# A two-layer pair kernel on one core: the second layer's projections in four row tiles, three blocks a set, with masking, channel order and output constants moved

## The reference, cut to what matters

```python
zn = _layernorm(z, ln_in_w, ln_in_b)
a = m * sigmoid(zn @ a_g_w.T + a_g_b) * (zn @ a_p_w.T + a_p_b)
b = m * sigmoid(zn @ b_g_w.T + b_g_b) * (zn @ b_p_w.T + b_p_b)
x = einsum('bikh,bjkh->bijh', a, b)
xn = _layernorm(x, ln_out_w, ln_out_b)
gate = sigmoid(zn @ g_w.T + g_b)
out = gate * (xn @ z_w.T + z_b)
```

## Time and profile before

| | us |
|---|---|
| Median of 3 runs | 320.16 |
| Lowest and highest | 319.91, 321.51 |
| The profiled execution | 320.25 |
| Its span in the trace | 318.4 |
| PE busy | 248.8 (78%) |
| DVE busy | 241.3 (76%) |
| ACT busy | 218.5 (69%) |
| POOL busy | 128.0 (40%) |

### The profile page before, as it was taken

One profiled execution on the slowest core, in us unless ns is written; L12 is line 12 of the kernel. 1 busy time (PEld: TensorE's weight loads), 2 busy tenths in 40 slices (PEclk: granted clock), 3 DMA queues, 4 the chain that ended last, 5 costly groups with the idle time before them and its releaser, 6 DMA issues.

```text
span 318.4 us, 7162 instructions
## 1 busy us (share of the span) xinstructions
PE 248.8 (78%) x2296; PEld 200.1 (63%) x2296; DVE 241.3 (76%) x543; ACT 218.5 (69%) x986; POOL 128.0 (40%) x140
## 2 busy tenths in 40 slices
PE   0597750589999999999999999998755977758710
PEld 0587320467778777887788787776555656658710
DVE  6058950578899888998989988887349479968994
ACT  1546650399998999998999989997445755426700
POOL 6670000045455455544554454555000365630562
PEclk9999595599999999999999999999758799978775
DMA  9100132635344354433544333410000462000017
GB/s 140 32 0 2 50 71 35 234 138 198 125 162 155 106 185 165 152 128 130 182 151 171 128 127 123 146 38 2 2 0 0 170 250 78 3 0 2 0 21 127
DMA packets 44041, 31.29 MB, mean 98 GB/s; under 512 B 23108, under 2 KB 44004, under 8 KB 44004
## 3 DMA queue, kind: packets, MB, share of 16 engines
q1 hardware_dynamic: 43004, 30.70, 30.5%
q10 hardware_dynamic: 1000, 0.13, 0.3%
HBM read 1.38 MB, written 1.18 MB: 8 GB/s over the span
## 4 chain that ended last, share of the span: by engine, by line
PE 64%; DVE 15%; DMA 6%; ACT 5%; issue 5%; SPq 2%; DVEq 0%; ACTq 0%
PE psum L1083 10%; PE psum L1135 10%; PE psum L1146 9%; PE psum L1086 5%; PE psum L1084 5%; PE psum L1115 5%; DMA maps<-mask_parts 4%; DVE tok L781 3%; PE psum L1001 3%; PE psum L979 2%; PE psum L1103 2%; PE psum L1204 2%; PE psum L1123 2%; DVE tok L836 2%; DMA maps<-in_x 2%
## 5 line engine op out<-in xcount | busy, mean ns | idle before, releaser
L497 POOL TENSOR_TENSOR probs<-probs,rden 96x384 f32<-96x384 f32 x96 | 79.0, 823 | 122.4 <-DVE rden L919 122.4
L645 ACT ACTIVATE probs<-psum,neg_max 96x96 f32<-96x96 f32 x384 | 124.1, 348 | 2.4 <-PE psum L1135 0.5
L645 ACT ACTIVATION_READ_ACCUMULATOR probs<-psum,neg_max 96x1 f32 x384 | 82.5, 215 | 0.0
L913 DVE COPY probs_t<-psum 96x384 f32<-96x384 f32 x96 | 52.9, 551 | 20.2 <-PE psum L1135 18.8
L882 DVE TENSOR_REDUCE neg_max<-psum 96x4 f32<-96x384 f32 x96 | 50.8, 529 | 2.0 <-PE psum L1086 2.0
L1083 PE MATMUL psum<-u_st,x_stack 128*96 128x384 f32 x96 | 40.5, 422 | 14.5 <-DMA u_st<-u_split 13.8
L1135 PE MATMUL psum<-ident,probs 96*96 96x96 f32 x384 | 47.7, 246 | 1.1 <-DVE probs_t L913 0.9
L1135 PEld LDWEIGHTS psum<-ident,probs 96*96 96x96 f32 x384 | 37.7, 126 | 5.4 <-issue 1.4
L1146 PE MATMUL psum<-probs_t,v_sb 128*32 128x96 f32 x768 | 35.8, 258 | 0.0
L1083 PEld LDWEIGHTS psum<-u_st,x_stack 128*96 128x96 f32 x96 | 15.7, 164 | 28.2 <-issue 14.0
L1086 PE MATMUL psum<-bias_lo,ident_r 128*96 128x384 f32 x96 | 33.0, 343 | 0.0
(11 more groups left out here) (167 smaller groups left out, 492.9 us busy)
## 6 DMA issues: line engine op xcount, KB each, us to landing
u_st<-u_split SPq DMA_DIRECT2D x96, 192.0 KB
x_stack<-shared SPq DMA_DIRECT2D x40, 96.0 KB, 2.1
x_stack<-bias_lo SPq DMA_DIRECT2D x10, 192.0 KB, 2.3
x_stack<-u_st SPq DMA_DIRECT2D x10, 192.0 KB, 2.3
maps<-in_x SPq DMA_DIRECT2D x4, 288.0 KB, 5.4
out_y<-maps SPq DMA_DIRECT2D x12, 96.0 KB, 2.2
x_stack<-shared SPq DMA_DIRECT2D x4, 192.0 KB, 2.3
bias_lo<-maps SPq DMA_DIRECT2D x24, 12.0 KB
```

The costliest lines, as they stand in the source:

```text
L497: pool.tensor_tensor(probs[:, m % SLOTS], probs[:, m % SLOTS], rden[:, m, :].unsqueeze(2).to_broadcast([N, H, N]), ALU.mult).then_inc(prob ...
L645: e = act.activation(probs[:, m % SLOTS, h], bank_s[m % 4][0:N, h * N:(h + 1) * N], ACT.Exp, bias=neg_max[:, m, h:h + 1], accum_out=den[:, ...
L913: dve.tensor_copy(probs_t[0:N, (m - T_BEHIND) % 2].rearrange("p h q -> p (h q)"), bank_t[0:N, 0:H * N]).then_inc(t_ready, 1)
```

## The change

All of it is for the second layer.

- A set is three blocks (`TRIO`), eight sets in all. Each of the four members has a bank of its own, 3 x 160 = 480 columns, and two groups of four banks alternate. PE writes the biases by four matmuls of 480 columns, then for each block four fp32 matmuls whose operands are 32 partitions deep, at partitions 0, 32, 64 and 96 (row tiles): `zn_t` of one member against that member's copy of the weights in `w_all`. The fp32r split of `zn`, its DMAs and the block-diagonal weights go.
- The mask is applied to the values instead of the gates, straight out of PSUM, into one of three `masked` buffers, one set ahead; ACT's sigmoids wait for it; the product of the two, now SBUF by SBUF, goes to `ab`. PE may write a set's banks again when all gates of set n - 2 are done.
- A block's values are ordered member first, channel innermost, so that the sums of squares read adjacent elements; the centring matmul reads its moving operand with a step. `ab` has its 64 channels innermost, so the triangle's operands step by 64 elements.
- Four transpose groups come ahead of set 0, the last two behind it.
- POOL's constants start when all gates are done: three pairs ahead of centring, three behind it.
- In the preparation the gate and value weights are no longer widened and spread on ACT: twelve small matmuls put a copy for each member, and the scale and shift in the new order, into `w_all`.

```diff
-        ab = shared[0:N, 0:2 * C * N].rearrange("k (t h i) -> k t h i", t=2, h=C)
+        ab = shared[0:N, 0:2 * C * N].rearrange("k (i t h) -> k i t h", t=2, h=C)
...
-        ZN_AHEAD = 3
+        ZN_AHEAD = 4
...
+        def projection_bank(n, f):
+            return banks[GROUP * (n % 2) + f]
...
-            for q in range(1, QUADS):
-                for k in range(COPIES):
-                    if k < 2:
-                        sp.wait_ge(zn_lo_ready if k else zn_hi_ready, q)
-                    sp.dma_start(x_stack[k:P:COPIES, :, 4 * q:4 * q + 4, :].bitcast(f32).rearrange("c f b j -> c f (b j)"),
-                                 (zn_lo if k % 2 else zn_hi)[:, q - 1].bitcast(f32)).then_inc(zn_stacked[q - 1], 16)
...
+            pool.wait_ge(gates_ready, 2 * SETS)
...
+            for q in range(CONST_EARLY):
+                gate_constant(q)
             pool.wait_ge(tri_mean_ready, 1)
             for n in range(CHUNKS // 2, CHUNKS):
                 center_chunk(pool, n).then_inc(last_centered, 1)
+            for q in range(CONST_EARLY, QUADS):
+                gate_constant(q)
...
+            for n in range(SETS):
+                if n == 1:
+                    for q in range(ZN_AHEAD, QUADS):
+                        zn_copy(q)
+                act.wait_ge(values_masked, n + 1)
+                need(act, ab_ready, n - 1)
+                act.activation(gates_ab[:, n % 2], projections(n, slice(0, VALUES * C)), ACT.Sigmoid).then_inc(gates_ready, 1)
+                act.activation(gate_sb[:, trio(n)].rearrange("j b f c -> j f b c"),
+                               projections(n, slice(VALUES * C, GATES * C)), ACT.Sigmoid).then_inc(gates_ready, 1)
...
+            def mask_values(n):
+                dve.wait_ge(proj_done, n + 1)
+                need(dve, ab_ready, n + 1 - MASKED)
+                dve.tensor_tensor(masked[n % MASKED], projections(n, slice(GATES * C, PW)),
+                                  mask_rows[:, :, trio(n)].unsqueeze(3).to_broadcast([N, GROUP, TRIO, VALUES * C]),
+                                  ALU.mult).then_inc(values_masked, 1)
+            mask_values(0)
+            for n in range(SETS):
+                if n + 1 < SETS:
+                    mask_values(n + 1)
+                dve.wait_ge(values_masked, n + 1)
+                dve.wait_ge(gates_ready, 2 * n + 1)
+                dve.tensor_tensor(ab.rearrange("k (f b) t h -> k f b (t h)", f=GROUP)[:, :, trio(n)],
+                                  masked[n % MASKED], gates_ab[:, n % 2], ALU.mult).then_inc(ab_ready, 1)
...
+                        if layer:
+                            mm = pe.matmul(to.rearrange("j (f c) -> j f c", f=GROUP), centered_t[:, 4 * q + n, :],
+                                           centering_r[:, :, :].rearrange("p c f -> p f c"), start=True, stop=True)
...
+            def project(n):
+                need(pe, gates_ready, 2 * (n - 1))
+                for f in range(GROUP):
+                    pe.matmul(projection_bank(n, f)[0:N, 0:TRIO * PW], ones_r[:, :],
+                              tri_b[:, None, 0:PW].to_broadcast([P, TRIO, PW]), start=True, stop=False)
+                for b in range(TRIO):
+                    for f in range(GROUP):
+                        at = slice(f * C, (f + 1) * C)
+                        mm = pe.matmul(projection_bank(n, f)[0:N, b * PW:(b + 1) * PW], zn_t[at, TRIO * n + b, :],
+                                       w_all[at, 0:PW], start=False, stop=b == TRIO - 1)
                 mm.then_inc(proj_done, 1)
...
+                if n == 1:
+                    for q in range(ZN_AHEAD, QUADS):
+                        block_transposes(q, 1, zn_ready)
                     pe.wait_ge(zn_ready, QUADS)
...
-                    mm = pe.matmul(banks[4 + b % 4][0:N, n * N:(n + 1) * N], ab[:, 1, h, :], ab[:, 0, h, :],
+                    mm = pe.matmul(banks[4 + b % 4][0:N, n * N:(n + 1) * N], ab[:, :, 1, h], ab[:, :, 0, h],
```

More of the change, by code:

```diff
@@ L348, in triangle_kernel, with projections, trio @@
         WEIGHT2_DMAS = 16 * (3 + len(tri_weights) + len(tri_biases))
[L350 to L358, removed]
+        def projection_bank(n, f):
+            return banks[GROUP * (n % 2) + f]
+        def projections(n, at):
+            first = GROUP * (n % 2)
+            outs = psum[0:N, first * BANK:(first + GROUP) * BANK].rearrange("p (f x) -> p f x", f=GROUP)[:, :, 0:TRIO * PW]
+            return outs.rearrange("p f (b c) -> p f b c", b=TRIO)[:, :, :, at]
+        def trio(n):
+            return slice(TRIO * n, TRIO * n + TRIO)
         def z_bank(q):
@@ L589, in first_copies @@
                 act.wait_ge(weights2_loaded, WEIGHT2_DMAS)
-                for n, w in enumerate((tri_in[:, :], tri_in2[:, :], wz_in[:, :])):
-                    rows = w.shape[0]
-                    act.activation(w_wide2[0:rows, n], w.unsqueeze(2).to_broadcast([rows, C, GROUP]),
-                                   ACT.Copy).then_inc(widened, 1)
+                act.activation(w_wide2, wz_in[:, :].unsqueeze(2).to_broadcast([C, C, GROUP]),
+                               ACT.Copy).then_inc(widened, 1)
             def second_diagonals(f):
@@ L780, in norm_front @@
                     dve.wait_ge(d_squared, QUADS * layer + q + 1)
[L781 removed]
+                    ins = dve.tensor_reduce(tok[:, 0, at], by_layer(work, layer)[:, at].rearrange("j b c f -> j b f c"),
                                             AX.X, ALU.add)
@@ L972, in fourfold, with to_groups @@
                 return pe.matmul(bank[:, at], w, moving, start=True, stop=True)
+            def to_groups(at, w, moving):
+                for f in range(GROUP):
+                    mm = pe.matmul(bank_w[f * C:(f + 1) * C, at], w, moving, start=True, stop=True)
+                return mm
             def wide(w):
@@ L1000, in norm_front @@
                     for n in range(4):
-                        mm = pe.matmul(banks[q][0:N, n * HD:(n + 1) * HD], centered_t[:, 4 * q + n, :],
-                                       centering_r[:, :, :].rearrange("p c f -> p (c f)"), start=True, stop=True)
+                        to = banks[q][0:N, n * HD:(n + 1) * HD]
+                        if layer:
+                            mm = pe.matmul(to.rearrange("j (f c) -> j f c", f=GROUP), centered_t[:, 4 * q + n, :],
+                                           centering_r[:, :, :].rearrange("p c f -> p f c"), start=True, stop=True)
+                        else:
+                            mm = pe.matmul(to, centered_t[:, 4 * q + n, :],
+                                           centering_r[:, :, :].rearrange("p c f -> p (c f)"), start=True, stop=True)
                     mm.then_inc(d_done, 1)
@@ L1019, in block_transposes @@
                 for n in range(4):
-                    mm = pe.transpose(banks[6 + q % 2][:, n * N:(n + 1) * N],
-                                      blocks_t[:, 4 * q + n].rearrange("p c f -> p (c f)"), ident[0:N, 0:N])
+                    src = (square[:, 4 * q + n].rearrange("p f c -> p (f c)") if layer else
+                           by_blocks(square)[:, 4 * q + n].rearrange("p c f -> p (c f)"))
+                    mm = pe.transpose(banks[6 + q % 2][:, n * N:(n + 1) * N], src, ident[0:N, 0:N])
                 mm.then_inc(transposed, 1)
```

136 lines of the change are left out of this document (41 added, 95 removed).

## The result

The changed kernel took 323.65 us in the median of 8 runs (322.43 to 325.36), the kernel before 320.38 in 8 runs beside it (318.50 to 321.51). The ratio is 1.0103 (interval 1.0072 to 1.0135): about 1% slower, where 315.4 and faster was forecast. The profiled execution took 323.57 and its span is 321.1, 2.7 more than before.

What follows compares the result with a forecast made beforehand. DVE was taken to bound the projections. From 320.25 us, Parts 1 to 4 gave -6.9, the triangle and preparation 0, the constants +2.0: 315.4 us, with a range of 311 to 323.5.

Steps and rivals of the forecast that it cites:

- Part 1: The centred map: sums of adjacent elements save 0.8 us; the centring matmuls' stepped reads priced at 0, bound 3.4 more.
- Part 5: The triangle: both operands step by 256 bytes, priced at 0, other bound some +1.8 us; clock left as it was.
- Part 2: Transposes and set 0: one set of bias and row-tile matmuls takes 2.2 us; set 0 ends at about 251.55.
- Part 3: The hole before set 1: PE idle some 2.7 us, then half the clock for most of set 1.
- Part 4: Sets 2 to 7 of the projections: period 2.25 us, triangle starting at 275.45; Parts 1 to 4 together -6.9 us.
- Part 6: POOL's constants: three pairs between centring and scaling delay the scaling, +2.0 us, fully on the path.
- Stepped reads slow PE: Rival for centring matmuls and triangle: stepped operands cost +3.4 and +1.8 us, giving 320.6, no change; chance 0.13.
- The tiles overlapped: Against the rival that row tiles take turns: tile part 3.2 us, set 4.4, time 332.5; its chance 0.13.
- the loads didn't queue: Against the rival that weight loads queue: tile part 1.9 us, set 3.05, time 321.7; its chance 0.12.
- the clock didn't hold: Against the rival that PE stays at 1.00 through the hole, triangle or both: 311.3 us; its chance 0.12.
- two tile rivals: Row-tile matmuls of the projections: weight loads queue (321.7 us, chance 0.12), or tiles do not overlap (332.5 us, chance 0.13).

Runs made afterwards that it cites:

- f_three: The changed kernel with the centring matrix in reading order, all transposes ahead of set 0 and four early constant pairs: 313.75 us, ratio 0.9816 to the kernel before.
- f_four: f_three with positions innermost in `ab` as well, so the triangle reads adjacent elements: 311.08 us, ratio 0.9727 to the kernel before.

## Why the prediction was wrong

**The step that failed** is "I take 0" for the stepped reads, in Part 1 and again in Part 5. The row for it was at hand (DVE, 1.00 against 0.70), and it was set aside with the argument that an fp32 instruction's two clock periods per column already hold a stepped element's time. A column of a stepped instruction takes 0.228 / 128 = 1.78 ns at either clock level; two periods at the high level are 0.84. The argument would have needed the stepped element's price to be under 0.84 ns, and DVE's row gave 1.95 for one. The bound beside it leaned on the wrong size too, a factor of nearly two on DVE: the rows give 1.00 against 0.70, 1.4. On PE it was 2.1 at the high level (0.228 against 0.109).

**Part 1.** The sums took 0.68 (0.70 forecast), and their -0.8 is there (0.7 in the kernel with the matrix in reading order). The step cost 4.3 us of PE where its bound was 3.4. The bound's split into some 16 slow and 32 fast instructions holds; it put the stepped ones at the half clock's 0.213, and all 48 took 0.228, which is 0.7 more. Together +3.6 instead of -0.8.

**Part 2.** Right. Four bias matmuls 1.11 (0.96), the tile part 1.07 (1.2 with the tiled mode's 0.3), a set 2.12 (2.2). No row showed the 0.3 for entering and leaving the tiled mode, and no run sets it apart; the two errors, 0.1 short and 0.1 over, cancelled by luck.

**Part 3.** Right: a PE hole of about 2.4 to 2.6 (2.7), and the clock fell in it. That the hole itself was worth 3.5 us stood in the working (2.7, and 1.65 for the clock), but the order that makes it was taken as given.

**Part 4.** Right: period 2.2 (2.25), mask and product 0.95 each (0.90, 0.95), granted clock 1.00 from 264 on. Reciprocal to triangle -6.5; forecast -6.1. What hid under the projections before was off the path, as said.

**Part 5.** It failed as Part 1 did. Its other bound was right: +1.8 as the bound, +1.9 measured.

**Part 6.** Right: +2.0 forecast, +2.3 measured. DVE's own wait for POOL was only 1.6 of it, because L834 just ahead took 0.80 beside POOL's constants instead of 0.21. What the part had missed is 0.7 us after: POOL, which had been running, took its next instruction 0.02 us ahead of DVE, and DVE's scaling took 1.57 beside it instead of 0.69. All seven traces with three early pairs have it so (POOL first by 0.02 or 0.03, DVE's scaling 1.56 or 1.57); in the other seven DVE was first and took 0.69.

**The sum.** 315.4, plus 4.4 (Part 1) and 1.9 (Part 5), plus 0.3 and 0.7 (Part 6), less 0.4 (Part 4) is 322.3. The remaining 1.3 of the profiled 323.57 is the first layer's end, 0.4 later, 0.3 behind the scaling, and 0.6 between span and time (2.47 against 1.85). The first layer's end varies by more than that from run to run, so nothing of it is put to the change.

**The rivals.** "Stepped reads slow PE" had the mechanism and gave 320.6; with the measured terms it would have been 321.7, since Part 1 came out 4.4 above the forecast and Part 5 1.9, where it had 3.4 and 1.8. The tiles overlapped, the loads didn't queue, and the clock didn't hold. The sets of the two tile rivals (3.05 and 4.4) are 0.2 above what their terms add up to (2.9 and 4.2), which changes nothing here. The rival of the stepped reads had 0.13, though a row spoke for it and only an argument against it. Yet with the odds turned around the forecast would have been 320.6, no change: the sign needed the measured price and the 1.0 of Part 6 as well.

**What stays open.** The terms of the first stage and the triangle are shown by undoing them. Four early constants were run only as part of f_three and f_four. By the medians f_three is 9.9 less than the changed kernel, of which two of its edits alone gave 8.4; that leaves 1.5 for four early pairs, where 3.2 was expected and six gave 1.8. In its trace DVE's scaling starts 25.2 after the triangle's start, against 26.8 with three pairs and 26.3 with six. So whether four are better than six isn't settled. Nor is what a stepped weight load costs at the high clock, or why the clock rises late.

## What to carry to other kernels

A layout that gives one engine adjacent elements takes them from another: before moving a step from DVE's read to PE's, look at whether those PE instructions run at the high clock, because steps of 16 and 128 bytes held them at the half clock's pace. A small matrix can be stored in the order in which it will be read, which costs one stepped write (0.34 us here, 0.29 without the step) and keeps both sides adjacent. A bound that a row supports shouldn't be priced at 0 by an argument; where one side has a row and the other a story, the row gets the larger chance.

## What the runs showed of the hardware that was not expected

- An fp32 matmul of 128 columns with a moving operand in steps of 16 or 128 bytes took 0.228 or 0.220 us at the granted clocks 0.50 and 1.00 alike (adjacent 0.213 and 0.109). In steps of 8 bytes it took 0.113 at the high level, 4% more than adjacent. Matmuls of 96 columns with both operands in steps of 256 bytes were no faster at 1.00 than at 0.50 either.
- PE reached its high level later, or not at all, with stepped reads, though its busy time was full in both cases. At L1001 the kernel before had 0.77 in the second stretch of 2 us, and the same kernel with 16 bytes still 0.50 in the third (the changed kernel 0.80 there). In the triangle the split is clean: in all seven kernels with a stepped operand the clock was at 0.50 from the third microsecond at the latest to the end, 10.7 or 10.8 us, even where it had started at 1.00; in the seven with adjacent elements it rose to 1.00 some 4 to 7 us after the start. But f_four, with adjacent elements at L1001, also had 0.50, 0.50 and 0.52 in the first three stretches, and paid 1.4 us for it (8.4 against 7.0), so at L1001 the step is not the only thing that decides it. What else does wasn't tried.
- On DVE a product of 768 elements whose write steps took 1.49 us and delayed the next instruction by 1.35; with adjacent elements 0.95. This was visible only in the distance between starts.
